# Tokens normed, routed and sent in four groups as attention's values arrive, and 36 expert tiles whose two halves each have an expert of their own

## The reference, cut to what matters

```
x = x + conv(group_norm(x))   # 32 sequential steps of a learned memory: 4 weight matrices per batch
                              # with momentum: m = eta*m - lr*grad ; p = (1-forget)*p + m
t = tokens(x)                 # 4 x 1024 tokens of 128 features
t = t + attention(norm(t))    # additive attention in a band of 32 neighbours, softmax, values = norm(t)
n = norm(t)                   # 4096 tokens
  logits = n @ Wr + br ; top 2 of 8 experts, weights = their softmax over the two
  xe = norm(n) * ln_g[e] + ln_b[e]
  y  = gelu(xe @ W1[e] + b1[e]) @ W2[e] + b2[e]        # 128 -> 512 -> 128
t = t + sum over the two experts of weight * y
```

## Time and profile before

| | us |
|---|---|
| median of 3 runs | 1100.88 |
| lowest and highest | 1100.43, 1101.18 |
| the profiled execution's own time | 1100.4 |
| its span, first to last instruction | 1098.3 |

### The profile page before, as it was taken

The page is one execution under the profiler, slowest core; times in us unless marked ns, Lnnn a source line. Parts: engine busy times, 40 slices in busy tenths (PEclk is TensorE's granted clock), DMA queues, the critical chain, the costliest instruction groups (busy, mean ns, idle before and its releaser), DMA issues. The chain is left out here.

```text
span 1098.3 us, 24794 instructions
## 1 busy us (share of the span) xinstructions
PE 782.3 (71%) x8328; PEld 495.6 (45%) x8328; DVE 708.8 (65%) x1763; ACT 559.6 (51%) x1159; POOL 570.7 (52%) x738
## 2 busy tenths in 40 slices
PE   2656888888888888888888598465590005999990
PEld 2345444544444444444444244213460004988970
DVE  0573688888888888888888725795864002555554
ACT  2444676667667766776676231682340002555540
POOL 0033567776776677667767494100005772554550
PEclk9775899999999999999999899676765557999995
DMA  9003900000000000000000130300001112222217
GB/s 208 0 1 73 118 0 0 0 0 0 0 0 0 0 0 0 0 0 0 0 0 0 38 117 0 95 1 0 4 1 34 53 53 55 76 72 70 70 52 236
DMA packets 58539, 39.22 MB, mean 36 GB/s; under 512 B 17904, under 2 KB 51336, under 8 KB 58496
## 3 DMA queue, kind: packets, MB, share of 16 engines
q1 hardware_dynamic: 52256, 28.53, 12.8%
q0 software_dynamic: 4544, 9.38, 2.5%
q10 hardware_dynamic: 1696, 0.72, 0.4%
HBM read 19.40 MB, written 16.66 MB: 33 GB/s over the span
## 5 line engine op out<-in xcount | busy, mean ns | idle before, releaser
L360 POOL TENSOR_TENSOR s_w<-l_kw,l_m 128x512 f32<-128x512 f32 x192 | 238.0, 1274 | 12.3 <-DVE l_m L510 12.3
L510 DVE SCALAR_TENSOR_TENSOR l_m<-l_m,l_eta,lp_g 128x256 f32<-128x256 f32 x512 | 219.6, 476 | 37.1 <-PE lp_g L626 26.0
L1257 ACT ACTIVATE f_hh<-fp_h 128x1024 f32<-128x1024 f32 x39 | 39.9, 1023 | 167.1 <-PE fp_h L1339 167.0
L1279 POOL DMA_INDIRECT f_yg<-f_yr,f_xmeta x78 | 74.8, 959 | 85.7 <-DVE f_yr L1497 73.5
L457 ACT ACTIVATE l_kw<-s_w,l_keep_lr 128x256 f32<-128x256 f32 x256 | 116.7, 506 | 0.0
L1274 POOL DMA_INDIRECT f_xg<-f_xrow,f_place x64 | 61.9, 967 | 63.7 <-DVE f_xrow L1454 44.4
L1489 DVE TENSOR_TENSOR f_hs_lo<-f_hh,f_hs_hi 128x1024 bf16<-128x1024 f32 x39 | 47.8, 1225 | 67.0 <-ACT f_hs_hi L1261 67.0
L1315 PE MATMUL fp_x<-f_identb,f_xt 128*128 128x128 bf16 x156 | 15.7, 226 | 94.6 <-DMA f_xt<-f_xg 94.6
L450 ACT COPY l_wt<-lp_b 128x512 f32<-128x512 f32 x96 | 56.4, 588 | 27.8 <-PE lp_b L619 27.8
L1478 DVE COPY f_xf<-fp_x 128x512 bf16<-128x512 bf16 x39 | 16.2, 415 | 81.0 <-PE fp_x L1315 80.8
L365 POOL TENSOR_TENSOR l_kw<-s_w,l_keep 128x512 f32<-128x512 f32 x64 | 65.2, 1040 | 0.1
(11 more groups left out here) (309 smaller groups left out, 2110.5 us busy)
## 6 DMA issues: line engine op xcount, KB each, us to landing
f_xt<-f_xg SPq DMA_DIRECT2D x39, 130.0 KB
f_xg<-s_pad SPq DMA_DIRECT2D x1, 4992.0 KB, 31.3
s_w<-f_yg SPq DMA_DIRECT2D x16, 256.0 KB, 4.1
xs<-in_x_dram SPq DMA_DIRECT2D x4, 512.0 KB, 9.6
s_w1r<-in_L_ffn_W_dram SPq DMA_DIRECT2D x8, 256.0 KB, 2.7
r_w<-in_L_ffn_W_dram SPq DMA_DIRECT2D x8, 256.0 KB, 3.2
out_dram<-s_x SPq DMA_DIRECT2D x8, 256.0 KB, 3.3
t_xsh<-t_xl SPq DMA_DIRECT2D x4, 448.0 KB, 3.5
```

The source lines that it names most:

```text
L360: nc.gpsimd.tensor_tensor(W[k][:, half(h), :], KW[k][:, half(h), :], M[k][:, half(h), :], ALU.add).then_inc(w_ready[k], 1)
L510: i = nc.vector.scalar_tensor_tensor(out=M[k][:, b, :], in0=M[k][:, b, :], scalar=eta[:, b:b + 1], in1=ps_g[b][:, 0:256], op0=ALU.mult, op ...
L1279: nc.gpsimd.indirect_dma_start(sb["yg"][:, :], bass.IndirectOffsetOnAxis(ap=xmeta[:, j, a, 0:1].bitcast(mybir.dt.int32), axis=0), yr[j % R ...
```

## The change

1. In `learn`, W20 is treated as the other weights: ScalarE computes KW20 = W20*keep (four more operations per step, between two feature copies), and VectorE's update is one tensor_tensor of 128 x 1024.
2. The experts' bias table moves into `read_out`: eight fp32 matmuls (24 x 512) at four places of TensorE's order and eight VectorE operations at the end. `read_out` also loads W1 through a ring of four and makes two small tables on GpSimd (`lim`, `job`).
3. The values of attention move into `experts` and are interleaved with norm, routing and sending of four groups of 8 token blocks. Each group has its own chain of small operations on 64 instead of 256 elements and its own 16 scatters. Square roots and the exponential are taken once per group on ScalarE.
4. Each expert has a region of 4096 slots in `xg`, so a place is known without the other groups' counts. `xg` grows from 9984 to 33792 rows, and the fill with it.
5. Tiles: 36 instead of 39, still 256 rows, but each half of 128 rows has its own expert and start, so SyncE loads each half by its own DMA from a register, and TensorE loads an owner for each half in h and in y. h runs with 128 columns: 32 matmuls instead of 16.

```diff
@@ learn
-                    dve.wait_ge(keep_in, t + 1)
-                    for b in range(B):
-                        dve.wait_ge(mom_ready, mom(t, n, b // 2))
-                        i = nc.vector.scalar_tensor_tensor(out=W[k][:, b, :], in0=W[k][:, b, :], scalar=keep[:, b:b + 1],
-                                                           in1=M[k][:, b, :], op0=ALU.mult, op1=ALU.add)
+                    dve.wait_ge(kept[k], t + 1)
+                    dve.wait_ge(mom_ready, mom(t, n, 1))
+                    nc.vector.tensor_tensor(W[k][:, :, :], KW[k][:, :, :], M[k][:, :, :], ALU.add).then_inc(w_ready[k], 2)
@@ read_out, TensorE
+                    if k in (3, 4, 6, 8):
+                        for e in range(...):            # two experts at each of the four places
+                            nc.tensor.matmul(ps_b[0:NSPLIT, 0:H], lnb3[...], w1[e % 4][:, :], start=e == 0, stop=e == E - 1)
@@ experts, SyncE
+                sp.wait_ge(owner_ready, 3)
                 sp.wait_ge(sent, 16 * 2 * NT)
                 for j in range(NJ):
-                    sp.dma_start(tile[j % RING][:, :, :], sb["xg"][SL * j:SL * j + SL, :]...)
+                    for a in range(2):
+                        first = nc.sync.value_load(start_i[0:1, 2 * j + a:2 * j + a + 1], ...)
+                        sp.dma_start(tile[j % RING][:, a, :], sb["xg"][bass.ds(first, 128), :])
@@ experts, GpSimd
-                for n in range(NT):
-                    for k in range(2):
+                for g in range(GR):
+                    pool.wait_ge(place_ready, 2 * g + 2)
+                    ...
+                    for i in range(GT):
+                        for k in range(2):                 # 16 scatters of a group
@@ experts, VectorE
+                masked(0); masked(1); valued(0); masked(2); valued(1)
+                for g in range(GR):
+                    spread(g)                # variances of the group, sums for the roots
+                    if 2 * g + 3 < NTB: masked(2 * g + 3)
+                    normed(g)                # 8 blocks
+                    if 2 * g + 2 < NTB: valued(2 * g + 2)
+                    remainder(g)
+                    routed(g)                # top two, weights, places
+                    if 2 * g + 4 < NTB: masked(2 * g + 4)
+                    if 2 * g + 3 < NTB: valued(2 * g + 3)
@@ experts, TensorE, h of a tile
-                        e = owner_of(j)
-                        for h in range(NH):
-                            p = ps_h[j % 2][:, SL * h:SL * h + SL]
+                        for a in range(2):
+                            e = owner_of(2 * j + a)
+                            for h in range(NH):
+                                p = ps_h[j % 2][:, SL * h + 128 * a:SL * h + 128 * a + 128]
                                 ...
@@ and y
-                        e = owner_of(i)
                         for a in range(2):
+                            e = owner_of(2 * i + a)
```

More of the change, by code:

```diff
@@ L1165, in experts @@
-        both, inc, slot = (buf(n, [128, E, NT]) for n in ("both", "inc", "slot"))
-        rst, lnb3, btab = sb["rst"], sb["lnb3"], sb["btab"]
-        over, tiles, ends, base = buf("over", [128, E, 16]), buf("tiles", [128, E]), buf("ends", [128, E]), buf("base", [128, E])
-        past, owner = buf("past", [128, NJ, E - 1]), buf("owner", [128, NJ])
-        owner_i = buf("owneri", [128, NJ], mybir.dt.int32)
-        mine = buf("mine", [128, NJ], BF16)
-        place = buf("place", [128, 2, NT], mybir.dt.int32)
+        e = sb["e"]
@@ new lines, in experts @@
+        lg, key, one, two, lg2 = (buf(n, [128, GT, E]) for n in ("lg", "key", "one", "two", "lg2"))
+        m1, mk, p1, p2 = (buf(n, [128, GT]) for n in ("m1", "mk", "p1", "p2"))
+        both, inc, slot = (buf(n, [128, E, GT]) for n in ("both", "inc", "slot"))
+        rst, btab, lim, job = sb["rst"], sb["btab"], sb["lim"], sb["job"]
+        carry = buf("carry", [128, E])
+        over, tiles, ends = buf("over", [128, E, 32]), buf("tiles", [128, E]), buf("ends", [128, E])
+        past, owner = buf("past", [128, HALVES, E - 1]), buf("owner", [128, HALVES])
@@ L1307, in _, with weights @@
[L1307 removed]
+                def weights(n):
+                    pe.wait_ge(am_ready, n + 1)
+                    if n >= 1:
+                        pe.wait_ge(at_ready, n)
+                    for b in range(B):
+                        nc.tensor.transpose(ps_am[:, 128 * b:128 * b + 128], am[n % 2][:, b, :], ident)
+                    nc.tensor.transpose(ps_tail, tails[n % 2][:, :], ident).then_inc(at_done, 1)
@@ new lines, in counts @@
+                def counts(g):
+                    pe.wait_ge(count_ready, g + 1)
+                    pe.wait_ge(id_ready, 2)
+                    flat = both[:, :, :].rearrange("p e n -> p (e n)")
+                    nc.tensor.matmul(ps_c, sb["cst"][:, C_LOW:C_LOW + 128], flat, start=True, stop=True).then_inc(count_done, 1)
+                    nc.tensor.matmul(ps_k, ones[:, :], flat, start=True, stop=True).then_inc(count_done, 1)
+                for n in range(2):
+                    weights(n)
+                    values(n)
@@ L1418, in _ @@
-                nc.vector.tensor_tensor(both[:, :, :].rearrange("p e n -> p n e"), one[:, :, :], two[:, :, :], ALU.add).then_inc(count_ready, 1)
-                dve.wait_ge(ex_ready, 1)
-                link(nc.vector.tensor_scalar(p1[:, :], p2[:, :], 1.0, None, ALU.add))
-                link(nc.vector.reciprocal(p1[:, :], p1[:, :]))
-                i32_of = [row[k][:, :, 128:129].bitcast(mybir.dt.int32) for k in range(2)]
-                link(nc.vector.tensor_tensor(p2[:, :], p2[:, :], p1[:, :], ALU.mult))
```

544 lines of the change are left out of this document (304 added, 240 removed).

## The result

The changed kernel takes 1175.08 us (median of 4 runs, 1172.37 to 1175.56) against 1100.66 beside it: a ratio of 1.0671, 95% interval 1.0653 to 1.069, so 74 us slower. 1166.5 was forecast, with a range of 1135 to 1190. The profiled execution has a span of 1173.3 us, 75.0 more than before.

A forecast was written before the change was run, and what follows sets the result against it. The prediction took TensorE's sequencer, loading owners and computing addresses in order, to bound the expert tiles. Terms -6 + 8 - 36.0 + 99.8 = +65.8 on the 1098.3 us span gave 1164.1, forecast as 1166.5 us, range 1135 to 1190.

The forecast's parts named there:

- The bound: Expert tiles before the change: TensorE's in-order sequencer has no slack in its 3.7 us per tile; array work is 3.4.
- Tiles: Expert tiles: four loads and four address sets make 6.8 us per tile (6.0 to 7.2), +99.8 us in all.
- The addresses: Expert tiles: each half's eight addresses, with matmul issue, take 1.0 to 1.1 us for h and 1.0 for y.
- The fixed part: Expert tiles' stretch outside the periods: 9.5 us to land, fill and drain, plus 1.3 for SyncE's loads and second DMA.
- Overlap: Softmax's end to scatter's end: four groups hide scatter behind values and routing, 119.7 us instead of 155.7, gain 36.0 (31 to 44).
- read_out: The read_out block: eight added bias matmuls at 0.86 us each and a VectorE tail of 1 to 3, +8 us (6 to 10).
- learn: The learn block: the shorter VectorE update gains only 0.2 us in each of 31 steps, -6 us (0 to -12).
- Fill: Filling xg with 3.4 times the rows: 206 us of DMA, over by 306 and needed at 790, no cost.
- Hidden loads: Rival, expert tiles: second loads run beside the array's queue, 4.9 us per tile, 1098 us in all; chance 0.07.
- The array sets the tile: Rival, expert tiles: register work costs the queue nothing, 3.4 us per tile, 1044 us in all; chance 0.05.
- The clock: Rival, expert tiles: the half-idle array's granted clock falls too, +0.5 us per tile, 1184 us in all; chance 0.08.
- The break-even: Expert tiles: the period at which the changed kernel would equal the kernel before, 4.97 us per tile.

The follow-up runs named there:

- two_loads: The kernel before the change, with each owner loaded twice ahead of h and of y (4 loads per tile, still two address sets): 1152.34 us.
- halved_h: The kernel before the change, with h in two halves of 128 columns (32 matmuls instead of 16) and one owner: 1106.73 us.
- one_owner: The changed kernel, with the first half's owner used for both halves, so 2 loads and 2 address sets per tile: 1076.33 us.
- before_kept: The kernel before the change, with the owner's register kept from h for y, so 1 load per tile instead of 2: 1097.36 us, ratio 0.9973.
- kept_owners: The changed kernel, with each half's register kept from h for y, so 2 loads per tile instead of 4, all 4 address sets: 1127.1 us.
- learn_only: The kernel before the change, with only the changed learn block: 1093.68 us, ratio 0.9933.
- fill_only: The kernel before the change, with xg of 33792 rows instead of 9984, all filled, only the first 9984 used: 1100.99 us, ratio 1.0008.

## Why the prediction was right, point by point

*The bound.* Right for the changed kernel, and shown: TensorE's sequencer sets a tile's time. two_loads adds register work alone, and the period grows by 1.34 us; halved_h adds the 128 columns, and it grows by 0.16; one_owner keeps columns, DMAs and regions and is 2.89 us shorter than the changed kernel. For the kernel before it holds less strictly than the prediction has it. There three bounds lie close together: the sequencer's 3.76 us, the gelu's chain at 3.6 and the array's 3.4, and the sequencer's relief in before_kept brought 3 us instead of 10 to 14. The change added register work only, so this did no harm.

*The sum.* Its terms give 1164.1 + 2.1 + 0.5 = 1166.7, where the prediction has 1166.5. By stage the misses are -2.7 (`learn` and before it), +3.7 (`read_out`), -0.3, +1.3, +6.8 (tiles) and +0.4 us, 9.2 in all; that the first two nearly cancel is luck.

*Tiles.* Forecast 6.8 us per tile, measured 7.02. The term that was too small is the load: I took 0.6 to 0.7 us each, and the runs gave 0.67 (two_loads) to 0.71 (kept_owners). `turn` was 0.1 in the sum, and from the last half of y (1004.33, about 1.0 of issue) to the next load at 1005.6 there are some 0.2. The addresses are right: a half takes 0.9 to 1.1 us with the matmuls between them, as forecast; net of the matmuls a set is 0.73 to 0.84. The fixed part was 262.4 - 36 x 7.02 = 9.7 against 10.8, and 0.8 us of SyncE's first register load stands ahead of the stretch. In all +106.6 instead of +99.8.

*Overlap.* -34.7 against -36.0. The first group's scatters start within 1.2 us of the forecast (33.8, forecast 32.6). That the last issue agrees to 0.2 is luck. By the prediction's own terms the fourth group is ready (96.3) before the third is sent, so the last of the 32 issues from the third group on starts at 76.6 + 31 x 1.27 = 116.0, not 117.4, and the gain would be 37.4. Measured, the third group starts at 839.07 - 760.94 = 78.1, 1.5 later than forecast, and 78.1 + 31 x 1.27 is the 117.6 seen. SyncE's first register load starts at 881.1, so the last scatter had landed by 120.2 after the softmax; the table's 121.0 has 0.8 us of that load in it.

*read_out.* This was the worst-sized term against its range, +11.7 against 8 (6 to 10). The matmuls:

```profile
631.32 1.90 PE L845 MATMUL rp_b<-r_w,r_lnb 128*24 128x512 f32 x4
633.14 1.98 PE L854 MATMUL rp_z<-r_g,r_wf 128*128 128x512 f32 x4
```

A pair takes 633.14 - 631.32 = 1.82 us, not 1.72, so 7.3 in all. TensorE's last matmul of the block comes 74.4 us after its start (684.52 - 610.16) against 65.5 before (684.34 - 618.85), +8.9, and VectorE's tail behind it is 2.8 us longer. That makes the 11.7. I had 6.9 and 1 to 3, whose sum is 7.9 to 9.9, and took its lower end. Of TensorE's 8.9 us the matmuls explain 7.3; no run explains the other 1.6.

*learn.* -7.4 measured alone against -6. From TensorE's first matmul of the first step to the block's end it is 509.7 us in learn_only and 509.7 in the changed kernel, against 517.2 before. In the changed kernel another 1.1 us comes ahead of that first matmul (100.51 against 101.63); fill_only and learn_only show 101.8 and 102.2 there, and no experiment explains it.

*Fill.* Nothing, as forecast.

*Rivals.* Hidden loads: refuted by two_loads, where not even unused ones are hidden. The array sets the tile: refuted, 3.4 us would have to be seen. The clock: the granted clock was 1.00 from 930 to 950 with the array busy 74% of the time, and 0.98 to 1.00 in every stretch read from 893 to 1144, so the gaps of 0.4 to 0.8 us did not lower it; only the start ran slow, 0.50 from 888 to 893, behind nearly 30 us in which TensorE had stood idle:

```profile
888.00:893.00 5.00, 4.84 (x45) 4.64 (x46) 0.43 (x2) 1.06 (x2) 0.00 (x0) 0.50 0.23 57
```

*The break-even* of 4.97 us per tile agrees with both sides: kept_owners, at 5.60, is slower than before (1127.1), one_owner, at 4.13, faster (1076.33). From the measured times it is 7.02 - (1175.08 - 1100.66) / 36 = 4.95.

## What to carry to other kernels

A share of busy time near 100% doesn't say that the array is the bound: compare equal groups of matmuls, and look at the sequencer's own rows for register loads and computed addresses. Price a second run-time index per tile by its loads and by every address that hangs on it, load each once, keep it in its register, and put the load ahead of the stage's wait. A change that hides one stage and lengthens another should be taken apart: here the same change with the old tiles was 1.7 to 4.0% faster than the kernel before, by where the loads and the bias table stand.

## What the runs showed of the hardware

- A value loaded from SBUF into a register on TensorE's queue costs 0.67 (two_loads) to 0.71 us (kept_owners) of issue time where the sequencer sets the pace, though its three instructions last 0.47 together, and it costs that when nothing uses it. The Trainium skill (Runtime: NRT & Kernel Launch, section "Instruction fetch mechanics") has about 200 ns for a register load; the load instruction alone took 302 here.
- A set of eight register-addressed operands costs 0.73 to 0.84 us net, an estimate from kept_owners against one_owner and halved_h; its eight instructions last 4 x 46 + 4 x 32 = 312 ns. A second group of matmuls with the same register and offsets has no such rows in the trace (144 of each kind in one_owner, 288 in the changed kernel).
- An owner's load behind a wait is exposed, 0.30 us per tile on average; ahead of the same wait it was hidden (4.05 against 3.75).
- The granted clock stayed at 1.00 (930 to 950 us) with the array 74% busy and four gaps of 0.4 to 0.8 us in every 7.
